# Flamingo gated block on one core: a first transfer on ACT's queue, and gathered rows added between the halves of a late unit

## The reference, cut to what matters

```python
x = x + tanh(g_xattn[0]) * xattn(layernorm(x), ctx, ctx)      # x, ctx: [16, 128, 512]
x = x + tanh(g_ffn[0])  * ffn(layernorm(x), router, experts, shared)

def xattn(q, k, v):    # 8 heads; rows of a head's 16 channels, softmax(q^T k / sqrt(d)) over 512 columns
    ...
def ffn(x):            # 2048 tokens
    probs = softmax(x @ w_router)                 # 16 experts
    topk_w, topk_ids = top_k(probs, 4);  topk_w /= sum(topk_w)
    moe = sum over the 4 experts of topk_w * (silu(x @ w_gate[e]) * (x @ w_up[e])) @ w_down[e]      # 256 wide
    shared = (silu(x @ w_sh_gate) * (x @ w_sh_up)) @ w_sh_down                                      # 1408 wide
    return moe + sigmoid(x @ w_sh_expert_gate) * shared
```

## Time and profile before

| | us |
|---|---|
| median of 3 runs | 1207.63 |
| lowest, highest | 1207.46, 1210.73 |
| time of the profiled execution | 1211.22 |
| span in its trace | 1209.5 |
| PE, DVE, ACT, POOL busy in the span | 1160.2, 731.5, 521.9, 604.8 |

### The profile page before, as it was taken

One profiled execution on the slowest core, in us unless ns is written; L12 is line 12 of the kernel. 1 busy time (PEld: TensorE's weight loads), 2 busy tenths in 40 slices (PEclk: granted clock), 3 DMA queues, 4 the chain that ended last, 5 costly groups with the idle time before them and its releaser, 6 DMA issues.

```text
span 1209.5 us, 21576 instructions
## 1 busy us (share of the span) xinstructions
PE 1160.2 (96%) x6036; PEld 782.3 (65%) x6037; DVE 731.5 (60%) x1086; ACT 521.9 (43%) x1055; POOL 604.8 (50%) x599
## 2 busy tenths in 40 slices
PE   3799999999999999999999999999999999999996
PEld 1344444444444447887888887888888888878885
DVE  6688888888888518664444533433343334338877
ACT  1488787888778732111111233333433333321110
POOL 3245555555454324047667445545645746138653
PEclk9999999999999999999999999999999999999998
DMA  9467677766676109944554255555554464433555
GB/s 237 130 181 193 186 208 187 200 188 193 185 197 189 42 35 363 382 142 166 205 196 165 88 173 192 165 200 173 183 189 165 160 205 164 148 98 106 163 171 185
DMA packets 104815, 214.58 MB, mean 177 GB/s; under 512 B 12352, under 2 KB 17472, under 8 KB 104768
## 3 DMA queue, kind: packets, MB, share of 16 engines
q1 hardware_dynamic: 85408, 152.08, 41.3%
q0 software_dynamic: 18016, 61.88, 15.5%
q10 hardware_dynamic: 1344, 0.04, 0.1%
HBM read 117.48 MB, written 91.75 MB: 173 GB/s over the span
## 4 chain that ended last, share of the span: by engine, by line
PE 61%; DVE 1%; issue 0%; ACT 0%; DVEq 0%
PE score_ps L138 19%; PE score_ps L1627 18%; PE d_ps L1651 9%; PE d_ps L1577 7%; PE score_ps L1603 3%; PE o_ps L1577 2%; PE d_ps L1641 1%; PE o_ps L1641 1%; DVE y_all L1425 1%; DVE y_all L1413 0%; DVEq L161 0%; DVE h_split L1446 0%; DVE th L1433 0%; DVE hid L1439 0%; ACT h_split L1237 0%
## 5 line engine op out<-in xcount | busy, mean ns | idle before, releaser
L673 DVE TENSOR_REDUCE maxima<-score_ps 128x2 f32<-128x1024 f32 x256 | 301.5, 1218 | 51.1 <-PE score_ps L779 47.1
L626 ACT ACTIVATE probs<-sb_ps 128x512 f32<-128x512 f32 x512 | 266.5, 596 | 59.5 <-PE sb_ps L806 58.3
L138 PE MATMUL score_ps<-yn_t,w_split 128*128 128x512 f32 x1056 | 254.6, 397 | 0.0
L1627 PE MATMUL score_ps<-w_split,x_split 128*128 x948 | 254.2, 405 | 0.0
L138 PEld LDWEIGHTS score_ps<-yn_t,w_split 128*128 128x128 f32 x1056 | 197.0, 188 | 51.3 <-issue 4.7
L806 PE MATMUL sb_ps<-q_stack,places 50*128 50x512 f32 x512 | 187.3, 469 | 7.7 <-DMA q_stack<-max_t 6.9
L779 PE MATMUL score_ps<-places,q_stack 48*128 48x512 f32 x512 | 168.8, 474 | 20.8 <-DMA q_stack<-q_dram 16.4
L1627 PEld LDWEIGHTS score_ps<-w_split,x_split 128*128 128x128 f32 x948 | 166.5, 189 | 26.5
L1140 POOL CAST w_split<-w_raw 128x1024 fp32r<-128x1024 f32 x63 | 67.2, 1067 | 211.1 <-POOLq L1212 134.8
L1142 POOL TENSOR_TENSOR w_split<-w_raw,w_split 128x1024 fp32r<-128x1024 f32 x63 | 152.1, 2415 | 5.2
L806 PEld LDWEIGHTS sb_ps<-q_stack,places 50*128 50x128 f32 x512 | 79.4, 188 | 105.9 <-ACT probs L626 67.2
(11 more groups left out here) (157 smaller groups left out, 1282.5 us busy)
## 6 DMA issues: line engine op xcount, KB each, us to landing
xs_dram<-zero SPq DMA_DIRECT2D x1, 20224.0 KB, 58.7
stage<-xs_dram SPq DMA_DIRECT2D x79, 256.0 KB, 2.8
res_dram<-stage SPq DMA_DIRECT2D x79, 256.0 KB, 2.0
places<-k_dram SPq DMA_DIRECT2D x64, 192.0 KB, 3.4
q_stack<-q_dram SPq DMA_DIRECT2D x64, 192.0 KB, 4.1
k_dram<-places SPq DMA_DIRECT2D x16, 512.0 KB, 2.8
q_dram<-places SPq DMA_DIRECT2D x16, 512.0 KB, 2.8
w_raw<-in_L_ffn_w_gate_dram POOLq DMA_DIRECT2D x16, 512.0 KB
```

The source lines that it names most:

```text
L138: mm = pe.matmul(dst[i], w[:, k, f * P:(f + 1) * P], self.yn_t[:, b, k, t * self.SPAN:(t + 1) * self.SPAN], start=(k == 0 and n == 0), sto ...
L626: act.activation(probs[:, c % 2, head(j)[2], :], sb_ps[:, bank_of_score(HG * c + j), :], ACT.Exp, scale=SCALE).then_inc(exp_done, 1)
L673: dve.tensor_reduce(maxima[q % 2][:, :].rearrange("p (h u) -> p u h", u=8)[:, u, :], sa_ps[:, pair_of_unit(q, g, u), :, :], AX_X, ALU.max) ...
L1627: mm = pe.matmul(gu_ps[j], x_split[j][:, b, k, :], w_split[:, bass.ds(at + (a * 3 * ex.PIECE + k * 2 * FE), 2 * FE)], start=(n == 0), stop ...
```

## The change

Two independent edits. The two DMAs of the first group's rows of maxima are taken out of SP's order and are issued by ACT, right behind its copy to `max_t` and ahead of its copy of the values. And in late units 1 to 7 one batch of gathered rows is added between the two halves of `hidden`; the rest of the unit's batches stays at its end. The numbers of batches become 1, 2, 2, 2, 2, 3, 3, 1 (before: 1, 2, 2, 2, 2, 2, 2, 3), so the last unit has its one batch between the halves and none at its end.

```diff
             load_rows(2, 0, True)
-            store_max_rows(0, 0)
...
+            def first_max_rows():
+                act.wait_ge(mt_done, 1)
+                for hf in range(2):
+                    act.dma_start(q_stack[0][64 * hf + ROWS:64 * hf + ROWS + 2, :, :].bitcast(F32),
+                                  max_t[16 * hf:16 * hf + 16, :].bitcast(F32)).then_inc(max_rows[0], 16)
...
                 act.activation(max_t[:, :], sb_ps[0:8 * HG, bank, 256:384], ACT.Copy).then_inc(mt_done, 1)
+                if isinstance(g, int) and g == 0:
+                    first_max_rows()
...
-    ADDED = (1, 2, 2, 2, 2, 2, 2, 3)
+    ADDED = (1, 2, 2, 2, 2, 3, 3, 1)
...
+        batches = [0]
...
-                b, since = t * TT + i, x - UNITS_A
-                if 0 <= since and b < sum(ADDED[:since + 1]):
+                b = t * TT + i
+                if b < batches[0]:
                     dve.wait_ge(added, 4 * b + 4)
...
-        def add_rows(b, x):
-
-            dve.wait_ge(acc_done, 4 * x)
+        def add_rows(units):
+
+            b = batches[0]
+            batches[0] += 1
+            dve.wait_ge(acc_done, 4 * units)
...
-        def hidden(c, t):
+        def hidden(c, t, between=None):
             for f in range(c.tiles):
                 y, i = c.tile(t, f), c.slot(t, f)
 
+                if f and between:
+                    between()
                 dve.wait_ge(th_done, y + 1)
...
             for t in range(NT):
-                hidden(c, t)
+                u, x = NT * (c.n - FIRST) + t, c.unit(t)
+                hidden(c, t, (lambda: add_rows(x - 1)) if u > 0 else None)
...
-                u = NT * (c.n - FIRST) + t
                 if u >= 0:
-                    for b in range(sum(ADDED[:u]), sum(ADDED[:u + 1])):
-                        add_rows(b, c.unit(t))
+                    for _ in range(ADDED[u] - (u > 0)):
+                        add_rows(x)
```

## The result

The changed kernel took 1203.16 us (median of 20 runs, 1200.44 to 1213.57) against 1209.84 us before (20 runs, 1206.70 to 1218.33). The ratio is 0.9948, 95% interval 0.9933 to 0.9963, so 4.5 to 8.1 us less. It is faster, as forecast: the interval is clear of 1, though the difference is half a per cent. It is 6.3 us instead of 10.1, and 1203.16 lies 1.9 us above the range. The median of the kernel before was 2.2 us above the one that the forecast started from.

The account below looks back on a forecast made before the run. The prediction took PE to carry 61% of the chain of waits, so gains lay where PE stood still or had finished. Terms 7.0 + 3.1 = 10.1 us, from 1207.63, gave 1197.5 us, range 1195.0 to 1201.3.

Parts of the forecast that it names:

- The tail: Last units: with no additions left at the end, DVE's last accumulation follows PE's last matmul; term -7.0 us.
- `hidden` of unit 7: Last unit on DVE: it starts 0.2 us late, since DVE's work in units 5 and 6 slightly exceeds PE's 16.67 us.
- `lower_hidden`: Unit 7 on DVE: it ends at 1192.0, 1.5 us before PE's last `down` at 1193.54, so PE doesn't move.
- DVE's end: After PE's last matmul: one accumulation of 0.74 us remains, so DVE ends at 1199.9 instead of 1206.9.
- the stores kept up: Span's end: stores run at 385 GB/s, so the whole 7.0 us count; rival at 264 GB/s, gain 4.9 + 3.1, 8%.
- POOL's split: Unit 2: DVE's additions collide with POOL's split, longest 2.69 us against a median of 0.75; 4 us allowed.
- The copies: First group's maxima: issued by ACT, the copies land earlier and PE goes on at 33.4 instead of 36.42; term -3.1 us.
- The first rival: First maxima: copies on ACT's queue land no earlier, or only by issue time (0 to 1 us); 1199.6 to 1200.6 us; 15%.
- The bounds: Second copy's landing: 31.3 at the quickest, gain 5.1 us; 36.6 if like ACT's own loads, a loss of 0.2.
- the middle between the landings of 2.0 and 7.3 us: Copies' landing time behind ACT's issue: the middle of the bounds was taken as 4.1 us, giving 33.4.

Follow-up runs that it names:

- the additions alone: Kernel before with only the batches of additions changed, the copies left in SP's order: 1202.1 us, ratio 0.994 to the kernel before.
- second execution: The changed kernel profiled once more, for a second trace: 1202.18 us with a span of 1200.4.
- copies-only run: Kernel before with only the two copies issued by ACT, additions as before: 1210.29 us, ratio 1.000 to the kernel before.
- the SP run with the short queue: Changed kernel, but SP issues the copies, ahead of x and ctx of batch 2 and the stack of group 3: 1197.05 us, ratio 0.9896.
- the one with all loads beside: Changed kernel, but SP issues group 3's stack and batch 2's x and ctx at the moment ACT issues the copies: 1199.26 us, ratio 0.9917.
- first execution of the changed kernel: The first profiled execution of the changed kernel, which lost some 9 us between 560 and 680 us.
- the run with ACT's short queue: Changed kernel, but SP loads batch 2's x and ctx and group 3's stack only after ACT's copies have landed: 1196.1 us, ratio 0.989.

## Why the forecast was wrong, and where it was right

**The tail, right.** The term was -7.0; it measured 7.2 in the trace, and the additions alone make 0.994. Taking PE's 1.93 us earlier start of unit 7 off, the steps read: `hidden` of unit 7 at 1182.39, on time (forecast 0.2 late); `lower_hidden` 1.85 us ahead of PE's last `down` (forecast 1.5); DVE's end at 1197.99 (1197.97); the span's end 2.4 us behind it (2.5), so the stores kept up. In unit 2, where I allowed 4 us for POOL's split, the four additions took 7.15 us instead of 3.27 (timeline of the second execution):
```profile
1098.07 7.15 DVE L1436 SCALAR_TENSOR_TENSOR y_all<-ring,w_top,y_all 128x512 f32<-128x512 f32 x4
```
Its batch 4 ended at 1116.5, counted with PE's shift 0.9 later than forecast, and nothing waited. What I had not seen is that the place between the halves is more than room for a batch: it fills a hole that DVE has anyway. The forecast had it in its rows as 1.19 us of idle time ahead of the second L1433; where it stayed open in four units of twelve additions, PE ended 4.1 us late.

**The copies, wrong.** The step that failed is "On its own queue they are not behind the backlog, but share the 16 engines with it"; its term, -3.1, measured 0.0 (the interval of the copies-only run is 2.2 us either way). The first rival (15%) was what happened. Shown: with SP's stacks queued in front, no packet of the copies ran until the stacks were nearly through (0 of 36 beside 456 and 479 in 4 us); with little in front, the same copies let PE go on 4.5 us earlier, from either queue (31.66 and 31.34); with loads issued between the two copies, the second ran behind x and ctx, though they were in the other queue. So what counted was the order of issue over both queues, to within about one transfer: where issues overlap in time, packets of both queues run mixed (4 beside 123 and 14 beside 175 above). In the changed kernel the stacks are in front of the first copy, and x, ctx and the values of batch 2 between it and the end of the second: ACT's first issue took 1.27 us, so the second began at 29.5, and PE waits for both. The 1 us of issue that the rival allowed was lost in the same way. Why the order holds over two queues, in the generation of descriptors or in the engines, these runs don't tell. The sum had a slip besides: 36.42 - 33.4 is 3.0, and the middle between the landings of 2.0 and 7.3 us that it started from is 4.7, not 4.1. Neither matters beside the step.

The bounds should have warned me: ACT's own loads had taken 6.1 to 7.3 us on busy engines, near the loads of SP beside them, and I explained it away by their number of packets. The trace of the kernel before had the order itself. SP and ACT issued eight loads in turn there, at 13.51 (SP), 13.64 (ACT), 13.98, 14.13, 14.46, 14.67, 15.11 and 15.23 us, and they landed in just that order over both queues, at 19.4, 19.7, 20.9, 21.1, 21.7, 22.1, 22.3 and 22.5, a load of 0.5 KB last. The rule of the Trainium skill that I set against this part ("DMA: Bandwidth & Descriptors", Issuing engines are not separate DMA queues) was right in saying that another issuer saves no more than issue time. The rule of the same page of the Trainium skill that I leaned on (Queues, rings and completion order: an engine takes its queues in turn, packet by packet) doesn't give this order by itself. A packet in that rule of the skill is a group of descriptors, typically 9 to 17 and at most 64. If each of the profile's packets is one descriptor, SP's 479 are some 30 for each of 16 engines (an estimate): two or three typical groups without one packet of the copies between them, but fewer than the largest group. So the order seen is not the turns that I forecast; whether the groups were that large or the copies' packets hadn't reached the engines, no run here decides.

**The numbers.** 1203.16 - 1197.5 is 5.7 us: 3.1 by the copies, 2.2 by the median of before, and some 0.3 left over (6.7 between the medians against 7.0), which is less than the interval and so stands for nothing. Of the kernel before a longer series gave 1209.84, not 1207.63, and the range had no room for that on its upper side.

**The two lengths of the attention part.** It is 422.2 to 422.8 us in seven of the eleven traces and 420.8 to 421.3 in the other four, which are both traces of the changed kernel, the SP run with the short queue and the one with all loads beside. The copies-only run, with the same attention code as the changed kernel, is among the long ones. The difference arises in the first 16 us behind the wait, and PE's speed makes it. The first two groups of eight L824 matmuls (the former L817), first in the second execution of the changed kernel and then in the copies-only run:
```profile
43.38 1.91 PE L824 MATMUL o_ps<-probs,v_t 128*17 128x512 f32 x8
48.29 1.05 PE L824 MATMUL o_ps<-probs,v_t 128*17 128x512 f32 x8
```
```profile
43.24 1.91 PE L824 MATMUL o_ps<-probs,v_t 128*17 128x512 f32 x8
48.76 1.91 PE L824 MATMUL o_ps<-probs,v_t 128*17 128x512 f32 x8
52.38 1.05 PE L824 MATMUL o_ps<-probs,v_t 128*17 128x512 f32 x8
```
In all four short traces the second group takes 1.05 us, in all seven long ones 1.77 to 1.91. The traces' record of the granted clock fits: its first entry is full speed (2.4 GHz), and it begins at 45.5 us in the one and at 51.0 in the other. Before that entry there is none, so that the clock was at its lower level (1.2 GHz) is read from the durations. PE was as slow before the wait already (0.79 us for one L786, the former L779, at 27 us in the second execution, against 0.50 at 46.5). Why the rise comes early in some executions wasn't looked into; it isn't the edit, since the same attention code had both. It moves 1.5 us between executions, half of what the copies were to save.

**Open.** It wasn't tried whether spreading each copy over more engines would help.

## What to carry to other kernels

A small transfer on the critical path should be placed by what is issued ahead of it on any queue, not by whose queue it is on: put it in front of the loads that nobody waits for. A wait should be costed with the data that are issued ahead of it at that moment, on all queues (here 0.84 MB ran in the 4 us in which the copies stood). And where an engine works past the end of the bounding one, count two chains: moving work away pays until the other is the later, and a good place for it is a hole that is there already.

## What the hardware showed unexpectedly

The DMA queues of SP and ACT behaved nearly like one, in order of issue, to within about one transfer. With loads in front the copies' 36 packets ran 4.0 to 6.8 us behind the first issue (first execution of the changed kernel); without them PE itself went on 3.0 to 3.4 us behind it. A copy of 8 KB, 16 rows long, took ACT 1.27 us to issue and the next 0.63, also where SP issued nothing beside them (the run with ACT's short queue). The additions with both inputs in SBUF took 1.8 us each on average beside POOL's split (four in 7.15 us) and 0.75 us beside its gathers. PE ran the first 9 to 15 us behind the wait at the lower speed, and when it sped up differed by some 5 us between executions of the same code.
